# Routing steps in one run, shared downs paired during the scatter, picks' shares behind the works, work 2's rows turned inside work 1

## What is computed

```
h = patches @ W.T + b
h = h + attention(layernorm(h))                    # layer 0, softmax within an image
h = h + moe0(layernorm(h))                         # shared expert + 2 of 8 experts, width 768
h = h + linear_attention(layernorm(h))             # layer 1, 12 heads
h = h + moe1(layernorm(h))                         # shared expert + 2 of 3 experts, width 384
# moe0: scores = sqrt(softplus(x @ gate_w)); top 2 of scores + bias; weights = scores / their sum
#       expert(x) = (silu(min(x @ w1, 10)) * clip(x @ w3, -10, 10)) @ w2
```

## Time and profile before

| | us |
|---|---|
| median of 3 runs | 633.2 (629.99 to 634.15) |
| profiled execution, its time | 635.24 |
| its span, first to last instruction | 633.6 |
| PE busy / DVE / ACT / POOL | 552.0 / 362.5 / 254.6 / 237.3 |
| mean granted TensorE clock | 0.902 of 2.4 GHz |

### The profile page before, as it was taken

One profiled execution on the slowest core, in us unless ns is written; L12 is line 12 of the kernel. 1 busy time (PEld: TensorE's weight loads), 2 busy tenths in 40 slices (PEclk: granted clock), 3 DMA queues, 4 the chain that ended last, 5 costly groups with the idle time before them and its releaser, 6 DMA issues.

```text
span 633.6 us, 10186 instructions
## 1 busy us (share of the span) xinstructions
PE 552.0 (87%) x3648; PEld 531.1 (84%) x3648; DVE 362.5 (57%) x871; ACT 254.6 (40%) x523; POOL 237.3 (37%) x182
## 2 busy tenths in 40 slices
PE   5899879987999999999991569298889979999997
PEld 5788879986999999999991558297779878999997
DVE  0566757447655555555541676975785656345554
ACT  0357341243444544544611224454544334333432
POOL 1404002743464664664724522744753300011300
PEclk9799878999899999999997688696878789799999
DMA  9720001744456656656422230000020100000001
GB/s 351 276 105 2 1 1 45 286 155 150 140 195 229 254 182 226 255 181 226 159 64 68 69 137 0 2 1 2 0 69 2 68 1 1 2 1 1 1 1 57
DMA packets 23623, 62.79 MB, mean 99 GB/s; under 512 B 6336, under 2 KB 16480, under 8 KB 20896
## 3 DMA queue, kind: packets, MB, share of 16 engines
q1 hardware_dynamic: 17504, 55.59, 24.5%
q0 software_dynamic: 1728, 3.54, 1.8%
q10 hardware_dynamic: 4352, 3.15, 1.5%
HBM read 53.32 MB, written 8.95 MB: 98 GB/s over the span
## 4 chain that ended last, share of the span: by engine, by line
PE 75%; DVE 14%; ACT 5%; issue 3%; DMA 2%; POOL 1%; SPq 0%; DVEq 0%; ACTq 0%
PE bank L611 23%; PE bank L628 12%; PE bank L411 9%; PE bank L431 6%; PE bank L1016 4%; PE bank L1030 3%; PE bank L766 3%; PE bank L847 2%; PE bank L988 2%; PE bank L787 2%; PE bank L752 2%; DVE Y L1521 2%; PE bank L1004 2%; DVE qkw L1875 1%; PE bank L1053 1%
## 5 line engine op out<-in xcount | busy, mean ns | idle before, releaser
L670 POOL TENSOR_TENSOR w0l<-stage,w0h 128x768 fp32r<-128x768 f32 x32 | 58.7, 1835 | 98.7 <-ACT w0h L654 88.8
L628 PE MATMUL bank<-w0d,a0h 128*128 128x192 f32 x492 | 83.0, 327 | 1.0 <-DVE H L730 1.0
L628 PEld LDWEIGHTS bank<-w0d,a0h 128*128 128x128 f32 x492 | 79.7, 191 | 1.3 <-DVE H L730 1.3
L709 DVE TENSOR_SCALAR a0t<-bank 128x256 f32<-128x256 f32 (+1 forms) x114 | 50.8, 445 | 47.7 <-PE bank L611 47.6
L681 ACT ACTIVATE bank<-bank 128x256 f32<-128x256 f32 x96 | 35.3, 368 | 97.5 <-PE bank L611 93.0
L668 POOL TENSOR_TENSOR w0t<-stage,w0t 64x768 fp32r<-64x768 f32 x32 | 58.4, 1824 | 13.7 <-ACT w0t L654 9.6
L611 PE MATMUL bank<-XWh,w0h 128*128 128x256 f32 x192 | 56.5, 294 | 6.9 <-DVE a0t L709 3.3
L611 PE MATMUL bank<-XWh,w0t 128*128 128x256 f32 x192 | 54.8, 285 | 0.0
L611 PE MATMUL bank<-XWl,w0h 128*128 128x256 f32 x192 | 54.8, 285 | 0.0
L611 PE MATMUL bank<-XWh,w0l 128*128 128x256 f32 x192 | 54.8, 285 | 0.0
L611 PE MATMUL bank<-XWl,w0t 128*128 128x256 f32 x192 | 54.7, 285 | 0.0
(11 more groups left out here) (253 smaller groups left out, 1376.6 us busy)
## 6 DMA issues: line engine op xcount, KB each, us to landing
stage<-moe0w SPq DMA_DIRECT2D x17, 1536.0 KB, 7.2
w0d<-moe0d SPq DMA_DIRECT2D x17, 576.0 KB, 4.0
stage<-moe1w SPq DMA_DIRECT2D x4, 1056.0 KB, 4.9
patch<-patches SPq DMA_DIRECT2D x4, 768.0 KB, 7.8
slots_in<-zero SPq DMA_DIRECT2D x4, 768.0 KB, 13.0
XR<-slots_in SPq DMA_DIRECT2D x16, 192.0 KB, 3.8
slots_out<-YO ACTq DMA_DIRECT2D x16, 192.0 KB, 2.5
XR<-slots_in SPq DMA_DIRECT2D x16, 64.0 KB, 3.8
```

Of the source, the lines that this page charges most:

```text
L628: last = nc.tensor.matmul(bank[e_bank(qpar, t, shared)][:, 0:D], A0["h"][qpar][:, fc, t * P:(t + 1) * P], W0[par]["down"][:, fc, :], start ...
L670: ins = engine.tensor_tensor(W0[par]["l"][:, mat, :], src, W0[par]["h"][:, mat, :].bitcast(F32), ALU.subtract)
L709: nc.vector.tensor_scalar(A0["t"][fc % 2][:, 0:width], bank[2 + fc % 2][:, 0:width], LIMIT, -LIMIT, ALU.min, ALU.max).then_inc(S0["clip_re ...
```

## The change

- PE: the router's tiles 6 to 8 come ahead of unit 2 of q = 0. Order of the shared expert: gate_up q0, r_sel wait and count matmuls, gate_up q1, down 0, down 1, gate_up q2, rows of work 1, down 2.
- DVE: clips and products of q = 0 are written out one by one. `scores`, `compare`, `choose` run with only clips 2 and 3 between them (inside `scores`), then product 2, clip 4, `bases` and `slots`, product 3, clip 5, product 4, `experts`, product 5.
- ACT: `high(1, 2)` moves ahead of the softplus, both after silu 1. Weight splits of work 1 move ahead of q = 2.
- Shared down tiles use banks 4, 5 and 6, two tiles to a bank, and are added in five additions (SHARED_ADD), four of them of two tiles. DVE's split of work 1's weights comes right after q = 1.
- The rows of work 2 are turned after unit 2 of work 1; ACT and DVE take them after their unit 3.
- `share` and `weights` move behind all works, behind the tau steps and ahead of `mixture`.

```
+SHARED_AT = ((4, 0), (4, 1), (5, 0), (5, 1), (6, 0), (6, 1), (4, 0), (4, 1), (5, 0))
+SHARED_ADD = ((0, 2, 4), (2, 4, 5), (4, 6, 6), (6, 8, 4), (8, 9, 5))
...
-                    d = 3 * q + t
-                    if d >= 2:
-                        pe.wait_ge(S0["acc_done"], d - 1)
+                    at, side = SHARED_AT[3 * q + t]
+                    dst = bank[at][:, side * D:(side + 1) * D]
+                    if q == 2 and side == 0:
+                        pe.wait_ge(S0["acc_done"], at - 3)
...
+            if isinstance(n, int) and n == 1:
+                pe.wait_ge(S0["acc_done"], 3)
...
             router(3 * D, E0, range(3, 6), rt_z)
-            e_gate_up(pe, 0, 0, 0, 0, range(2, 3))
             pe.wait_ge(ln_lo, 12)
             router(3 * D, E0, range(6, 9), rt_z)
-            e_gate_up(pe, 0, 0, 0, 0, range(3, FC0))
-            e_gate_up(pe, 1, 0, 0, 1, range(2))
+            e_gate_up(pe, 0, 0, 0, 0, range(2, FC0))
...
-            e_gate_up(pe, 1, 0, 0, 1, range(2, FC0))
+            e_gate_up(pe, 1, 0, 0, 1)
             e_down(pe, 0, 0, 0, 0, True, 16)
+            e_down(pe, 1, 1, 0, 0, True, 16)
             e_gate_up(pe, 2, 0, 0, 2)
-            e_down(pe, 1, 1, 0, 0, True, 16)
+            e_rows(pe, 1, 1, 32)
             e_down(pe, 2, 0, 0, 0, True, 16)
-            e_rows(pe, 1, 1, 32)
...
+                if isinstance(n, int) and n == 1:
+                    e_gate_up(pe, n + 2, n, par, None, range(3))
                     e_rows(pe, n + 1, 1 - par, x_loaded)
+                    e_gate_up(pe, n + 2, n, par, None, range(3, FC0))
...
-            e_act(act, 0, CHW, None, None, None, {1: last_high, 2: softplus})
+            e_act(act, 0, CHW, None, None, None, {1: softplus})
             e_act(act, 1, CHW, None, None, None)
+            for i in range(4):
+                e_split_act(act, 1, 1, i, 32, None)
             e_act(act, 2, CHW, None, None, None)
-            for n in (1, 2):
-                for i in range(4):
-                    e_split_act(act, n, n % 2, i, 16 * n + 16, None if n == 1 else 2)
-            act.wait_ge(x_T, 1)
-            nc.scalar.activation(XWh[1][:], bank[6][:], ACT.Copy).then_inc(x_hi, 1)
-
-            e_act(act, 3, WT, None, (2, 0, None), None)
+            for i in range(4):
+                e_split_act(act, 2, 0, i, 48, 3)
+            e_rows_high(act, 1, 1, None)
+
+            e_act(act, 3, WT, None, None, None, {3: lambda: e_rows_high(act, 2, 0, None)})
...
                                                op1=ALU.min).then_inc(rt_neg, 1)
+                e_clip(dve, 0, 2, CHW)
                 dve.wait_ge(rt_e, 1)
...
                                                op1=ALU.add).then_inc(rt_sp, 1)
+                e_clip(dve, 0, 3, CHW)
                 dve.wait_ge(rt_sc, 1)
...
-            e_dve(dve, 0, 0, CHW, None, None, None,
-                  {1: lambda: low(1, 2), 2: scores, 3: lambda: compare(u, E0), 4: choose})
-            e_dve(dve, 1, 1, CHW, None, None, lambda: e_acc(dve, 0), {1: placed, 2: experts})
-            e_dve(dve, 2, 0, CHW, 3, None, lambda: e_acc(dve, 1))
+            for fc in range(2):
+                e_clip(dve, 0, fc, CHW)
+                e_product(dve, 0, 0, fc, CHW)
+            low(1, 2)
+            scores()
+            compare(u, E0)
+            choose()
+            e_product(dve, 0, 0, 2, CHW)
+            e_clip(dve, 0, 4, CHW)
+            bases()
+            slots()
+            e_product(dve, 0, 0, 3, CHW)
+            e_clip(dve, 0, 5, CHW)
+            e_product(dve, 0, 0, 4, CHW)
+            experts()
+            e_product(dve, 0, 0, 5, CHW)
+            e_dve(dve, 1, 1, CHW, None, None, None)
             e_split_low(nc.vector, dve, 1, 1)
-            e_acc(dve, 2)
...
+            for i in range(3):
+                e_acc(dve, i)
+            e_dve(dve, 2, 0, CHW, 3, None, None)
+            e_rows_low(dve, 1, 1)
+            for i in range(3, 5):
+                e_acc(dve, i)
+            e_dve(dve, 3, 1, WT, 6, None, None, {3: lambda: e_rows_low(dve, 2, 0)})
+            e_dve(dve, 4, 0, WT, 9, (3, 1), lambda: e_copy(dve, 1, 1, None))
...
+            share(sc, E0, comb[:], True)
+            weights()
```

More of the change, by code:

```diff
@@ L619, in e_down, with e_bank @@
                 if shared:
-                    d = 3 * q + t
-                    if d >= 2:
-                        pe.wait_ge(S0["acc_done"], d - 1)
-                elif isinstance(n, int) and n == 1:
-                    pe.wait_ge(S0["acc_done"], 8 + t)
-                else:
-                    pe.wait_ge(y_done, n * 2 + (t - 3))
+                    at, side = SHARED_AT[3 * q + t]
+                    dst = bank[at][:, side * D:(side + 1) * D]
+                    if q == 2 and side == 0:
+                        pe.wait_ge(S0["acc_done"], at - 3)
+                else:
+                    dst = bank[e_bank(t)][:, 0:D]
+                    if isinstance(n, int) and n == 1:
+                        pe.wait_ge(S0["acc_done"], len(SHARED_ADD))
+                    else:
+                        pe.wait_ge(y_done, n * 2 + (t - 3))
                 for fc in range(FC0):
-                    last = nc.tensor.matmul(bank[e_bank(qpar, t, shared)][:, 0:D],
-                                            A0["h"][qpar][:, fc, t * P:(t + 1) * P], W0[par]["down"][:, fc, :],
+                    last = nc.tensor.matmul(dst, A0["h"][qpar][:, fc, t * P:(t + 1) * P], W0[par]["down"][:, fc, :],
                                             start=(fc == 0), stop=(fc == FC0 - 1))
                 last.then_inc(S0["down_ready"], 1)
-        def e_bank(qpar, t, shared):
-            return 4 + ((qpar + t) % 2 if shared else (1 + t) % 2)
+        def e_bank(t):
+            return 4 + (1 + t) % 2
         def e_rows(pe, n, par, loaded):
             pe.wait_ge(ld_x[par], loaded)
-            if not (isinstance(n, int) and n == 1):
+            if isinstance(n, int) and n == 1:
+                pe.wait_ge(S0["acc_done"], 3)
+            else:
                 pe.wait_ge(x_lo, n - 1)
@@ L689, in e_act, with e_rows_high @@
             if rows is not None:
[L690 to L694, removed]
+                e_rows_high(act, *rows)
+        def e_rows_high(act, n, par, used):
+            act.wait_ge(x_T, n)
+            if used is not None:
+                act.wait_ge(S0["gu_ready"], used)
+            nc.scalar.activation(XWh[par][:], bank[6][:], ACT.Copy).then_inc(x_hi, 1)
         def e_store(act, n, par):
@@ L707, in e_dve @@
             for fc in range(FC0):
[L708 to L715, removed]
+                e_clip(dve, q, fc, width)
+                e_product(dve, q, qpar, fc, width)
                 if fc in between:
@@ L718, in e_dve, with e_rows_low, e_acc @@
             if rows is not None:
[L719 to L722, removed]
+                e_rows_low(dve, *rows)
             if before is not None:
                 before()
[L726 to L731, removed]
+        def e_rows_low(dve, n, par):
+            dve.wait_ge(x_hi, n)
+            nc.vector.tensor_tensor(XWl[par][:], bank[6][:], XWh[par][:].bitcast(F32),
+                                    ALU.subtract).then_inc(x_lo, 1)
+        def e_acc(dve, i):
+            t0, t1, at = SHARED_ADD[i]
+            dve.wait_ge(S0["down_ready"], t1)
+            nc.vector.tensor_tensor(H[:, t0:t1, :], bank[at][:, 0:(t1 - t0) * D].rearrange("p (t d) -> p t d", d=D),
+                                    H[:, t0:t1, :], ALU.add).then_inc(S0["acc_done"], 1)
         def e_copy(dve, n, par, stored_):
@@ L738, in e_copy @@
                 dve.wait_ge(S0["down_ready"], n * 2 + (8 + t))
-                nc.vector.tensor_copy(YO[par][:, t, :], bank[e_bank(0, t, False)][:, 0:D]).then_inc(y_done, 1)
+                nc.vector.tensor_copy(YO[par][:, t, :], bank[e_bank(t)][:, 0:D]).then_inc(y_done, 1)
         @block.tensor
@@ L1197, in _, with softplus @@
             high(1, 1)
-            def last_high():
+            def softplus():
                 high(1, 2)
-            def softplus():
                 act.wait_ge(rt_neg, 1)
```

27 lines of the change are left out of this document (17 added, 10 removed).

## The result

The changed kernel takes 623.55 us (median of 4 runs, 623.15 to 624.19) against 631.6 (4 runs, 629.32 to 634.15): ratio 0.990, interval 0.985 to 0.994, about 1% faster. The two profiled executions took 635.24 and 623.15, so the profile has 12.1 us to explain, more than the 8.1 of the medians: before's profiled execution lies 3.6 us above its median. A table of stages places them. Each mark is the start of an instruction in the timelines: t12, the last transposes ahead of the router's tiles 3 to 5; the first matmul of the first shared down; work 1's and work 3's first matmuls; the mixture.

A forecast was written before the change was run, and what follows sets the result against it. PE was taken to bound the kernel, with 75% of the chain. Gains of 0.2, 1.85 and 6.5 us sum to 8.55, taking the median from 633.2 to 624.7 us, range 621.0 to 630.0.

The forecast's parts named there:

- Part 3: Work 2's rows turned inside work 1, shares behind the works: 6.5 us gained from work 1 to work 3.
- The reading from the steady work: Works 1 and 2 should take 7.82 and 11.72 us, sum 19.54, against 26.08 before.
- 0.5 for small gaps: In works 1 and 2: what was left of the 6.5 us gain beside holes and low clock.
- The price of nothing for DVE's copy within work 1: DVE's extra copy of 0.7 us in work 1 was charged nothing; 0.5 us if its cover is gone.
- (b): Work 2: something else stands behind the shares, the 3.30 us stays; gain 5.2, time 628.0; chance 0.10.
- (c): Behind the works: the shares are not hidden, ten steps take 17 us; time 633.2; chance 0.03.
- Part 2: Paired downs during the scatter: from down 0 to work 1, 1.85 us gained, bounds 1.2 and 2.6.
- The new wait before down 2: Down 2, right behind its own q = 2, waits for all six products: 0.8 us.
- Part 1: Routing in one run: q = 1 ends at 109.3 against 109.51, +0.2 us, bounds +0.8 and -0.9.
- the router's last matmuls no longer wait behind unit 2: In the router: z comes one low-clock unit of 3.22 us earlier, at 80.3 instead of 83.56.
- Rival (a): New holes keep the clock low through all of q = 1; gain 2.7, time 630.5; chance 0.08.
- Rival (d): DVE and ACT stretch the scatter by 17 us, deciding from 12; slower, 638.3; chance 0.04.

The follow-up runs named there:

- the third profile of after: The changed kernel, unaltered, measured and profiled again beside the kernel before: 623.05 us, ratio to before 0.988.
- part 1 alone: The kernel before with only the routing in one run (router's tiles 6 to 8 ahead of unit 2): 645.21 us, ratio to before 0.999.
- parts 2 and 3: The changed kernel with the old routing between the units; paired downs, work 2's earlier rows and late shares kept: 623.09 us, ratio to before 0.990.
- fill: The changed kernel with unit 2 of q = 0 between the router's last groups again, with its silu, clip and product: 622.61 us, ratio to before 0.989.
- before once more: The kernel before, unaltered, measured again for a second profile: 628.88 us, beside 631.13 us of the same kernel on the same chip, ratio 0.998.
- part 3 alone: The kernel before with only the shares behind all works and work 2's rows turned inside work 1: 620.99 us, ratio to before 0.987.
- after once more: The changed kernel, unaltered, measured again on another chip for its second profile: 624.1 us, ratio to before 0.991.
- the last mix: The changed kernel with routing steps spread between the units again and down 2 waiting product by product: 620.97 us, ratio to before 0.985.
- the second group: Four kernels measured on one chip, all slower than on the other chips; the kernel before took 644.15 us beside them.
- mix: The changed kernel with routing spread in another order (unit 2 between router groups, clips 4 and 5 before choose): 626.36 us, ratio to before 0.972.
- the third group: Later measurements on a chip of their own, looking again at the stretch before down 0; the kernel before took 631.13 us there.

## Why the prediction was right, and where it was not

**Total.** 624.7 was forecast, 623.55 came; 8.55 us less was forecast, 8.05 came. Of the three terms two were right and one was right only for the execution that I had read. That the total fits so well is in part luck: the same comparison on two other chips gave 5.3 and 8.1, and the 2.56 us behind the mixture were in no term.

**Part 3: right.** 6.5 forecast, 6.4 measured, 19.37 to 19.42 us in every profile with part 3 on every chip. Of the 6.4, 1.45 is the low clock behind the old hole, which came in three of four profiles that have the hole; without it the part is worth 4.9 (24.33 - 19.4). The reading from the steady work (7.82 + 11.72) was the right one. The 26.08 beside it takes a piece of the chain (166.79) for work 3's first matmul, which starts at 166.49: the stage was 25.78, and the forecast's "0.5 for small gaps" is 0.2. In part 2 the same slip is 0.16 (109.51 for 109.35). The price of nothing for DVE's copy within work 1, and for the shares behind the works, held: no idle time of PE in works 1 to 3, 5.92 us of DVE idle before the mixture (about 6 forecast). Rivals (b) and (c) fall with it.

**Part 2: right.** 1.85 forecast, 1.80 measured. The new wait before down 2 is 0.88 (0.8 forecast). Splitting the wait by product takes it away: 28.41 instead of 29.53 from down 0 to work 1. This 1.80 is read in the stage; no whole time parts it from the noise on a chip without stalls.

**Part 1: the step that failed is its +0.2 with bounds +0.8 to -0.9.** Against the profiled execution it measured +0.55 (or +0.02 in the third profile of after), within the bounds.

But what the part does to the kernel is another number, because the same code of before takes 33.6 in three of four profiles and the changed one 36.06 to 36.61 in three of three, and 35.93 with part 1 alone. In whole times it is not clear of noise: without part 1 the median is 1.0 us less (parts 2 and 3), with fill 0.4 us less. So 2.5 us is what single executions show, and no average. Where the clock comes back early (the 0.77 and 1.00 of the windows above), part 1 costs 2.5 us (36.06 against 33.6), or 2.1 by parts 2 and 3 without it (33.99), of which 0.2 comes back by the rows' load. Where it stays low up to 86 us it costs nothing: 36.63 and 36.61.

My working took its durations from an execution of the second kind, with units of 3.22 us that hide the hole of 1.80 us; what failed is the term "the router's last matmuls no longer wait behind unit 2", booked as a gain, when unit 2 was what PE had to do while ACT and DVE made the last tiles. Fill, which puts unit 2 back together with its silu, clip and product, shows it: no hole, low clock gone after 3.4 us, 2.9 us less. Whether the hole also keeps the clock low is not shown. The three profiles that have it stayed low for 10.2 us, where 3.4, or 13.6 and more, came without it; and the runs don't part the hole from the narrow router matmuls beside it.

**Rival (a)** came in a small form: in the profile of after the low level is back at 88.1 and 98.4, 3.4 us each, behind the holes of 1.81 and 1.96, not through all of q = 1.

**Rival (d): at most in a small size.** Of the 18 issues three behind the first took 1.18 to 1.62 us instead of 0.96 (before, one did, 1.18), the longest beside DVE's splits at 111.56 and 112.63: 25.2 us instead of 24.4, 0.8 of stretch where 12 would decide. The Trainium skill (SBUF — State Buffer, Who interferes with whom) says that a VectorE operation with two SBUF inputs and a GpSimd operation that reads SBUF exclude each other for a whole instruction, from which the forecast estimated up to 3.8 us. The trace shows 1.1 us over three issues, and one of them, at 103.66, came ahead of the splits. The row of 1.66 us that the forecast gives for the rule has one SBUF input and is not what the rule speaks of; the row that agrees is a later step, with two inputs, which ends 0.1 us behind POOL's split (timelines of DVE and POOL before), and takes 0.23 behind the works:

```profile
156.05 1.72 DVE L1557 TENSOR_TENSOR comb<-rt,rsum 128x72 f32<-128x72 f32 x1
```
```profile
155.88 1.80 POOL L668 TENSOR_TENSOR w0t<-stage,w0t 64x768 fp32r<-64x768 f32 x1
```

**What the total does not tell.** By the stages, the change is worth 4.9 to 6.4 by part 3 and 1.8 by part 2, less 0 to 2.5 by part 1: 4.2 to 8.2 us. The four comparisons of medians (8.05, 5.3 and 8.1, and 5.8 against before once more) lie in that span.

Whether the 2.56 us behind the mixture are chance is open. With one and the same code there, the fourteen profiles run from 283.2 to 287.9, and part 3 alone has 283.2, fill 286.5. But all three profiles of after have 283.2 to 283.7, and the two of before 286.3 and 287.5. Nor do TensorE's low stretches there lie at random: one begins 53.3 us behind the mixture in both profiles of before and lasts 13.6, in after and after once more it begins at 50.7 and lasts 17.1.

What decides whether the clock comes back near 75 us or only at 86 in a given execution stays open. It goes with how the run began: the six profiles without a low stretch near 25 us all had the clock back by 83 us, the three with the longest one there (some 6.8 us, from 25 to 32: before, after's third, and the last mix) all stayed low to 86; with 3.4 us there both came (three back by 85, two at 88, these two on the stalling chip). No run changed only that. Among profiles that began alike, part 1 costs 1.9 to 2.5 us in the first kind (33.60 and 33.99 against 35.93 and 36.06), nothing in the second (36.63 against 36.61), and 2.5 in the third (33.6 against 36.08) if the stalling chip is left out.

## What to carry to other kernels

- Before you price a move by one profile, look whether PE was at its low clock in that stretch. Matmuls at the low level (3.22 against 1.76 us for a unit here) hide the waits of their neighbours; add up the stage at both levels, with the waits that the high level lays open.
- A unit of matmuls between two dependent groups may be there to cover the copies between them. Moving it out to start a chain earlier pays only if the chain's end is late for someone: here `idx` came over 7 us earlier and bought 0.2 us.
- Take the start of a stage from the first instruction's own row; a piece of the chain can start later (166.79 for 166.49), and the difference goes into the sum.
- Elementwise steps whose result is used much later belong where their engine waits anyway; in the middle of a steady loop they cost their own time and, in three of four profiles, the low clock behind the hole (4.7 us for 3.30 of hole).

## What was not expected of the hardware

On the chip of the second group engines stood still during the scatter without a wait that the profile explains. With part 1 alone DVE stopped for 9.30 us, put down to "remote", which names no engine of this core, and PE for 11.11 behind it (timelines of DVE and of PE):

```profile
109.64 0.56 DVE L714 TENSOR_SCALAR a0t<-bank 128x384 f32<-128x384 f32 x1 [3.06 <-remote]
120.22 0.62 DVE L750 TENSOR_TENSOR H<-bank,H 128x192 f32<-128x192 f32 x2 [9.30 <-remote]
```
```profile
120.63 4.21 PE L633 MATMUL bank<-w0d,a0h 128*128 128x192 f32 x12 [11.11 <-DVE H L750]
```

In mix PE had many short stops, each inside a row of matmuls that wait for nobody:

```profile
111.16 1.08 PE L633 MATMUL bank<-w0d,a0h 128*128 128x192 f32 x5 [0.38 <-issue]
112.60 0.74 PE L633 MATMUL bank<-w0d,a0h 128*128 128x192 f32 x3 [0.36 <-issue]
114.01 0.34 PE L613 MATMUL bank<-X,w0l 128*128 128x384 f32 x1 [0.50 <-issue]
```

From down 0 to work 1 these four profiles took 33.24 to 45.47 us instead of 28.4 to 31.4, so 5 to 14 us more. The kernel before was 13 us slower there than in the third group (644.15 and 631.13); no profile of it was taken on that chip, so that this is the same thing is likely and not shown. They begin where the weight loads and the scatter run together: with part 1 alone the window from 105 to 110 us has the DMA engines busy 1.02 (mean share) at 426 GB/s. The same load, 1.04 at 429 GB/s, on another chip stopped nothing, and the longest stop lies where that load was gone (windows with part 1 alone, columns as in the earlier trace rows):

```profile
110.00:115.00 5.00, 0.00 (x0) 0.00 (x0) 0.82 (x2) 0.13 (x1) 3.78 (x5) 0.77 0.34 121
115.00:120.00 5.00, 0.00 (x0) 0.00 (x0) 0.00 (x0) 0.00 (x0) 2.00 (x3) 0.50 0.17 59
```

A rival is that the engines waited for their instructions, which have DMA queues of their own in the profile (q8 and q14). It would fit the releaser "issue" of the short stops, but from 104 to 122 us these queues carried no packet with part 1 alone. The cause stays open.
